# Window attention kernel: the running maxima enter the score matmuls through a free bias row instead of a product of their own

## The reference, cut to what matters

```python
xn = layernorm(x in channels-last)                 # 8 x 32 x 32 pixels, C = 64
win = xn in windows of 8 x 8                       # 128 windows of 64 tokens
q, k, v = (win @ w_qkv + b_qkv) split in 8 heads of depth 8
attn = (q * 8 ** -0.5) @ k.T + rel_bias_table[REL_IDX]   # bias by head, query and key
attn = softmax(attn, axis=-1)                      # over the 64 keys
out = (attn @ v) @ w_proj + b_proj
x1 = x + out, then layernorm, MLP, and the gated convolutions
```

## Time and profile before

| what | value |
|---|---|
| median of 3 runs | 324.87 us (323.93 to 325.02) |
| the profiled execution, its time | 324.21 us |
| its span in the trace | 322.4 us |
| PE busy | 289.2 us, 90% |
| DVE busy | 235.0 us, 73% |
| ACT busy | 203.0 us, 63% |
| POOL busy | 107.3 us, 33% |
| attention steps 0 to 7 | about 33 to 182 us of the span |

### The profile page before, as it was taken

The page is one execution under the profiler, slowest core; times in us unless marked ns, Lnnn a source line. Parts: engine busy times, 40 slices in busy tenths (PEclk is TensorE's granted clock), DMA queues, the critical chain, the costliest instruction groups (busy, mean ns, idle before and its releaser), DMA issues.

```text
span 322.4 us, 6206 instructions
## 1 busy us (share of the span) xinstructions
PE 289.2 (90%) x2314; PEld 211.3 (66%) x2314; DVE 235.0 (73%) x456; ACT 203.0 (63%) x343; POOL 107.3 (33%) x144
## 2 busy tenths in 40 slices
PE   2648979999999999999989797898999999999993
PEld 2236766878878686886868543453577777777772
DVE  4867437589798888979787336679999999976211
ACT  6696633948667685865535788987953746754400
POOL 4151425756576567555441601231310000000000
PEclk9986989999999999999979999999999999999998
DMA  6870383434244333424430000590008659767811
GB/s 162 178 156 31 84 188 85 104 76 90 71 98 89 78 84 76 103 67 96 101 71 2 0 2 0 115 212 14 2 0 169 130 113 196 141 137 147 182 33 33
DMA packets 17276, 29.94 MB, mean 93 GB/s; under 512 B 5536, under 2 KB 12192, under 8 KB 17248
## 3 DMA queue, kind: packets, MB, share of 16 engines
q1 hardware_dynamic: 13792, 22.72, 30.9%
q0 software_dynamic: 2880, 6.03, 11.0%
q10 hardware_dynamic: 576, 0.81, 1.0%
HBM read 4.22 MB, written 2.10 MB: 20 GB/s over the span
## 4 chain that ended last, share of the span: by engine, by line
PE 76%; DVE 7%; ACT 5%; SPq 4%; DMA 4%; issue 2%; POOL 0%; DVEq 0%; ACTq 0%
PE psum L1089 27%; PE psum L868 13%; PE psum L791 5%; PE psum L865 5%; PE psum L884 5%; PE psum L1013 3%; PE psum L844 3%; DVE maxima L1209 3%; SPq L379 3%; PE psum L1001 3%; PE psum L813 3%; DMA k_heads<-k_parts 3%; PE psum L892 2%; PE psum L818 2%; PE psum L823 2%
## 5 line engine op out<-in xcount | busy, mean ns | idle before, releaser
L1089 PE MATMUL psum<-shifted,conv_w 128*128 128x512 f32 x336 | 86.5, 419 | 0.0
L1089 PEld LDWEIGHTS psum<-shifted,conv_w 128*128 128x128 f32 x336 | 63.9, 191 | 21.6 <-issue 1.3
L868 PEld LDWEIGHTS psum<-q_heads,k_blocks 128*128 128x128 f32 x384 | 56.1, 194 | 6.5 <-issue 3.0
L868 PE MATMUL psum<-q_heads,k_blocks 128*128 128x256 f32 x384 | 57.3, 286 | 0.0
L1209 DVE TENSOR_REDUCE maxima<-psum 128x8 f32<-128x512 f32 x64 | 40.1, 683 | 12.2 <-PE psum L844 12.0
L603 ACT ACTIVATE probs<-psum 128x512 f32<-128x512 f32 x64 | 37.5, 603 | 18.2 <-PE psum L868 18.0
L461 POOL DMA_DIRECT2D k_blocks<-k_parts x56 | 32.2, 583 | 11.5 <-PE psum L868 11.5
L865 PE MATMUL psum<-minus_max,pick 128*128 128x512 f32 x64 | 32.7, 511 | 0.5 <-ACT probs L603 0.3
L844 PE MATMUL psum<-k_heads,q_blocks 128*128 128x256 f32 x128 | 24.0, 314 | 9.5 <-DMA k_heads<-k_parts 6.9
L791 PE MATMUL psum<-parts,center_average 128*128 128x512 f32 x64 | 22.6, 436 | 8.7 <-DVE parts L287 7.1
L287 POOL TENSOR_TENSOR parts<-x,parts 128x256 fp32r<-128x256 f32 (+1 forms) x21 | 19.4, 938 | 32.0 <-ACT parts L552 22.2
(11 more groups left out here) (142 smaller groups left out, 468.1 us busy)
## 6 DMA issues: line engine op xcount, KB each, us to landing
shifted<-images SPq DMA_DIRECT2D x32, 332.5 KB, 5.5
q_heads<-q_parts SPq DMA_DIRECT2D x128, 32.0 KB, 2.2
k_blocks<-k_parts POOLq DMA_DIRECT2D x56, 64.0 KB
k_heads<-k_parts SPq DMA_DIRECT2D x64, 32.0 KB, 2.3
out<-x SPq DMA_DIRECT2D x8, 256.0 KB, 4.8
q_blocks<-q_parts POOLq DMA_DIRECT2D x28, 64.0 KB, 2.5
x<-in_x SPq DMA_DIRECT2D x6, 256.0 KB, 6.2
x<-in_x SPq DMA_DIRECT2D x4, 128.0 KB, 4.0
```

The source lines that it names most:

```text
L868: ins = pe.matmul(bank[:, hh * G // 2:(hh + 1) * G // 2], k_blocks[:, hh, w // (NW // 2), k_part, w % (NW // 2), :], of_half(q_heads[:, q_ ...
L1089: ins = pe.matmul(psum[:, CONV0 + bh, :], conv_w[bh][:, w_part, t, :], img[:, y:y + H - 1:2, x0:x0 + W], start=t == 0 and w_part + part == ...
```

## The change

Of each bias row the bias of the last key is subtracted (from all keys alike, for each query), on both sides: in the rows for the maximum pass and in those for the scores. The row of the last key is then zero and is not needed. It holds the maxima of the query now, rounded to the format of the matmul operands, with weights of -1, 0 and 1 in `k_blocks`, such that each half of the 128 keys gets minus its own batch's maximum.

- The `pick` matmul of each `scores` and its constant are gone, and so are `maxima_t` and `minus_max`.
- The maxima are transposed in two halves of four window pairs: 32 columns each. The first transpose stands ahead of maximum pass 6, the second where the only one stood. DVE rounds either half into `gauge` by one copy of 32x128 (after the fifth maximum, and after the eighth).
- `send_gauge` places a half by two DMAs, 16 pieces of 512 bytes each, into the one free row of either half of `q_heads`. ACT issues the first half's after exponential 7, POOL the second half's after the second `key_blocks`. scores(g, 0) and scores(g, 4) wait for them.
- `q_heads` and `q_parts` have another order in memory: high and low part of a window pair lie side by side, so that a piece of a query DMA is one of 2048 bytes and not two of 1024.
- In the start there is one more load, `rel_base`: the base biases for all 128 partitions, in 1024 pieces of 256 bytes, 256 KB, on SP's queue ahead of the raw weights. DVE subtracts them (one instruction more, and one changed from a copy to a subtraction). POOL's making of `pick` is replaced by four small memsets.

```diff
+def _key_rows():
+    r = ((_p % T)[:, None] == T - 1 - _p % T).astype(np.float32)
+    r[_p % T == 0] = -(_p >= T).astype(np.float32)
+    return r
...
+        def maxima_bank(s):
+            return psum[0:32, MAX0, 0:128] if s else psum[0:32, PV, 256:384]
...
-        def reversal():
-            return const("reverse").unsqueeze(1).to_broadcast([128, NW, 128])
+        def reversal(name="reverse"):
+            return const(name).unsqueeze(1).to_broadcast([128, NW, 128])
+        FREE_ROWS = ((0, T), (1, 0))
+        def send_gauge(engine, n, s):
+            engine.wait_ge(S["dv_gauge"], 2 * n + s + 1)
+            if isinstance(n, int) and n == 0:
+                engine.wait_ge(S[f"q_heads_set{s}"], 1 + s)
+            else:
+                engine.wait_ge(S["pe_scores"], NW * (n - 1) + (s + 1) * NW // 2)
+            for hh, row in FREE_ROWS:
+                engine.dma_start(q_heads[row:row + 1, s, heads_of(hh)].rearrange("o h w l t -> o (h w) (l t)").bitcast(F32),
+                                 gauge[hh * 16:(hh + 1) * 16, s, :].bitcast(F32)).then_inc(S[f"gauge_in{s}"], 16)
...
             load_bias(1, "rel_table")
+            sp.dma_start(rel_base.rearrange("p (a f) -> p a f", a=WS), bass.AP(d["rel_table"].tensor, d["rel_table"].offset, [[0, 128], [side * NH, WS], [1, WS * NH]])
+                         ).then_inc(S["rel_in1"], 16)
...
                 sp.wait_ge(S["dv_q_low"], n + 1)
-                some = slice(half * G // 2, (half + 1) * G // 2)
+                some = slice(half * NW // 2, (half + 1) * NW // 2)
                 for h in range(NH):
-                    sp.dma_start(of_head(q_heads, h)[:, :, h, some].bitcast(F32), of_head(q_parts, h)[:, n % 2, :, some].bitcast(F32)
+                    sp.dma_start(of_head(q_heads, h)[:, half, h].rearrange("p w l t -> p (w l t)").bitcast(F32), of_head(q_parts, h)[:, n % 2, some].rearrange("p w l t -> p (w l t)").bitcast(F32)
...
             pool.memset(gaps[:], 0.0).then_inc(S["zeroed"], 1)
-            pool.wait_ge(S["consts_in"], 16)
-            pool.wait_ge(S["center_in"], 16)
-            pool.tensor_tensor(pick[:], const("average").unsqueeze(1).to_broadcast([128, NW, 128]),
-                               const("window_of_row").unsqueeze(2).to_broadcast([128, NW, 128]), ALU.mult).then_inc(S["po_pick"], 1)
+            pool.wait_ge(S["k_blocks_zeroed"], 1)
+            pool.wait_ge(S["zeroed"], 1)
+            for hh, row in FREE_ROWS:
+                for bh, sign in ((0, -1.0), (1, 1.0)):
+                    if hh + bh > 0:
+                        pool.wait_ge(S["key_rows_set"], 2 * hh + bh)
+                    pool.memset(k_blocks[row:row + 1, hh, :, 1, :, bh * T:(bh + 1) * T].bitcast(F32), sign).then_inc(S["key_rows_set"], 1)
...
                     key_blocks(nxt, 1 - par, 1)
+                    send_gauge(pool, nxt, 1)
...
             low_of_next_x(2)
+            send_gauge(pool, 0, 1)
...
                 exponentials(g, 7)
+                if nxt is not None:
+                    send_gauge(act, nxt, 0)
...
             late_bias(1, rel_low)
+            send_gauge(act, 0, 0)
...
-            def transpose_maxima(n):
-                pe.wait_ge(S["dv_max"], NW * (n + 1))
-                pe.matmul(psum[0:C, MAX0, 0:128], maxima[:], const("ident"), start=True, stop=True).then_inc(S["pe_maxt"], 1)
+            def transpose_maxima(n, s):
+                pe.wait_ge(S["dv_max"], NW * n + (s + 1) * NW // 2)
+                if s == 0 and not (isinstance(n, int) and n == 0):
+                    pe.wait_ge(S["dv_turned"], 2 * n - 1)
+                pe.matmul(maxima_bank(s), maxima[:, s * 32:(s + 1) * 32], const("ident"), start=True, stop=True).then_inc(S["pe_maxt"], 1)
-                if w == 0:
-                    pe.wait_ge(S["dv_minus"], g + 1)
                     pe.wait_ge(S["k_blocks_in0"], 64 * (g + 1))
+                    if isinstance(g, int) and g == 0:
+                        pe.wait_ge(S["key_rows_set"], 4)
                     pe.wait_ge(S[f"q_heads_in{w // (NW // 2)}"], 16 * NH * (g + 1))
+                    pe.wait_ge(S[f"gauge_in{w // (NW // 2)}"], 32 * (g + 1))
                 bank = psum[:, PROB0 + w % 2, :]
-                pe.matmul(bank, pick[:, w, :], minus_max[:, :, :], start=True, stop=False)
                         ins = pe.matmul(bank[:, hh * G // 2:(hh + 1) * G // 2], k_blocks[:, hh, w // (NW // 2), k_part, w % (NW // 2), :],
-                                        of_half(q_heads[:, q_part], hh)[:, :, w * T:(w + 1) * T], start=False, stop=hh + k_part == 2)
+                                        q_heads[:, w // (NW // 2), heads_of(hh), w % (NW // 2), q_part, :],
+                                        start=k_part + q_part == 0, stop=k_part == 1)
-            def weighted_values(g, quad, par):
+            def weighted_values(g, quad, par, nxt=None):
+                if quad == 1 and nxt is not None:
+                    pe.wait_ge(S["dv_gauge"], 2 * nxt + 1)
...
                         for w in windows:
+                            if w == 6:
+                                transpose_maxima(nxt, 0)
...
                 if nxt is not None:
-                    transpose_maxima(nxt)
+                    transpose_maxima(nxt, 1)
                     variance2(prev)
-                weighted_values(g, 1, par)
+                weighted_values(g, 1, par, nxt)
...
             for w in range(NW):
+                if w == 6:
+                    transpose_maxima(0, 0)
             queries(1)
-            transpose_maxima(0)
+            transpose_maxima(0, 1)
             keys(1)
-            pe.wait_ge(S["po_pick"], 1)
...
-            def high_of_bias(n, rel, done):
-                dve.wait_ge(S[f"rel_in{n}"], 32)
-                dve.tensor_copy(rel.rearrange("p (h a b) -> p h a b", h=NH, a=WS), patches(n)).then_inc(S[done], 1)
-                dve.wait_ge(S[done], 1)
-            def low_of_bias():
-                high, low = (t.rearrange("p (h a b) -> p h a b", h=NH, a=WS) for t in (rel_high.bitcast(F32), rel_low))
-                dve.tensor_tensor(low, patches(1), high, ALU.subtract).then_inc(S["dv_rel_low"], 1)
+            def square_rows(t):
+                return t.rearrange("p (h a b) -> p h a b", h=NH, a=WS)
+            def keys_bias():
+                dve.wait_ge(S["rel_in0"], 32)
+                rows = patches(0)
+                dve.tensor_tensor(square_rows(rel_flipped), rows, rows[:, :, WS - 1:WS, WS - 1:WS].to_broadcast([128, NH, WS, WS]),
+                                  ALU.subtract).then_inc(S["dv_rel_flipped"], 1)
+                dve.wait_ge(S["dv_rel_flipped"], 1)
+            def queries_bias():
+                dve.wait_ge(S["rel_in1"], 48)
+                dve.tensor_tensor(square_rows(rel_whole), patches(1), rel_base.rearrange("p (a b h) -> p h a b", a=WS, b=WS),
+                                  ALU.subtract).then_inc(S["dv_rel_whole"], 1)
+                dve.wait_ge(S["dv_rel_whole"], 1)
+                dve.tensor_copy(rel_high, rel_whole).then_inc(S["dv_rel_high"], 1)
+                dve.wait_ge(S["dv_rel_high"], 1)
+                low_part(dve, rel_whole, rel_high, rel_low).then_inc(S["dv_rel_low"], 1)
...
                 dve.wait_ge(S["ac_q_high"], n + 1)
-                dve.scalar_tensor_tensor(q_parts[:, par, 1, :], psum[:, MISC0, :], q_bias[:, 0:1],
-                                         q_parts[:, par, 0, :].bitcast(F32), ALU.add, ALU.subtract).then_inc(S["dv_q_low"], 1)
+                dve.scalar_tensor_tensor(q_parts[:, par, :, 1, :], by_window(psum[:, MISC0, :]), q_bias[:, 0:1],
+                                         q_parts[:, par, :, 0, :].bitcast(F32), ALU.add, ALU.subtract).then_inc(S["dv_q_low"], 1)
                 dve.wait_ge(S["pe_max"], NW * n + w + 1)
-                dve.tensor_reduce(maxima[:, w * NH:(w + 1) * NH], max_bank(w).rearrange("p (h t) -> p h t", t=T),
+                dve.tensor_reduce(maxima[:].rearrange("p (s h w) -> p s w h", s=2, h=NH)[:, w // (NW // 2), w % (NW // 2), :], max_bank(w).rearrange("p (h t) -> p h t", t=T),
-            def spread_maxima(n):
-                dve.wait_ge(S["pe_maxt"], n + 1)
-                dve.tensor_scalar(maxima_t[0:C, :], psum[0:C, MAX0, 0:T], -1.0, None, ALU.mult)
-                dve.tensor_scalar(maxima_t[C:128, :], psum[0:C, MAX0, T:2 * T], -1.0, None, ALU.mult).then_inc(S["dv_maxt"], 1)
-                dve.wait_ge(S["dv_maxt"], n + 1)
-                dve.tensor_tensor(minus_max[:], maxima_t[:].unsqueeze(1).to_broadcast([128, NH, T]),
-                                  const("head_of_row").unsqueeze(2).to_broadcast([128, NH, T]), ALU.mult).then_inc(S["dv_minus"], 1)
+            def round_maxima(n, s):
+                dve.wait_ge(S["pe_maxt"], 2 * n + s + 1)
+                if not (isinstance(n, int) and n == 0):
+                    dve.wait_ge(S[f"gauge_in{s}"], 32 * n)
+                dve.tensor_copy(gauge[0:32, s, :], maxima_bank(s)).then_inc(S["dv_gauge"], 1)
...
```

(14 more changed lines are left out.)

33 lines of the change are left out of this document (17 added, 16 removed).

## The result

| what | before | after |
|---|---|---|
| median of the runs (20 of each) | 323.75 us | 323.68 us (319.16 to 325.55) |
| ratio | | 0.9942, 95% [0.9915, 0.997] |
| the profiled execution, its time | 324.21 us | 320.28 us |
| its span | 322.4 us | 318.5 us |
| PE busy | 289.2 us | 280.9 us |

Ratios leave out executions more than 1.5% above the fastest of the same kernel: six of the twenty here (324.00 to 325.55 us; with them the means are 322.90 and 324.02 us, 0.35% apart), two of six in the second measurement, one without the base load, and one of 1419 us without the gauge DMAs.

What follows compares the result with a forecast made beforehand. PE and DVE were taken as one loop bounding each step, PE nearly alone. Steps save 7.7 us, the start costs 1.3: 324.2 - 7.7 + 1.3 = 317.8 profiled, plus 0.66 gives a 318.4 us median; range 311.8 to 322.5.

Steps and rivals of the forecast that it cites:

- so 0.9 are saved: Whole step, PE up to the weighted values: five products gone, 1.15 us, less 0.25 given back because ACT limits the scores.
- the five products' 1.15: PE between keys product and weighted values in a whole step: five removed products at 0.23 us each.
- ACT's copy of the residual: Whole step: normalising waits for ACT's residual copy and deviation; residual 0.84 us earlier, so normalising starts at about 13.21.
- the 1.45 us that I gave to steps 0 and 1: Gains of the first two steps: 0.35 us in step 0, behind the last key DMA, and 1.1 in step 1.
- I took 0.66 as before: Whole kernel: the median lies 0.66 us above the profiled execution, so 317.8 becomes 318.4 us.
- The base load: Start: 256 KB on SP's queue delay the first key DMAs and all behind them; cost 1.3 us, bounds 0 to 1.54.
- The gauge DMAs: Steps: ACT's two issues, at most 1.2 us, fit its 1.69 us of idle time ahead of the keys copy; no cost.
- The late-gauge rival: First half lands after 4.4 us, scores 0 start 1.5 us late in seven steps; 325.5 us, about no change; chance 0.05.
- DVE's copies: Steps, on DVE: two copies of 32x128 replace the three spreading instructions, 0.25 us each, bounds 0.22 and 0.69.
- Steps 6 and 7: Last two steps: 1.3 us net saved in step 6, where nothing is normalised, and 1.6 in step 7, which runs on PE.
- The clock rival: PE's clock falls in its longer pauses, about 1.7 us lost in each of six steps; 328.5 us, slower; chance 0.11.
- a wait of 0.7 ahead of the fourth pass: Sign in the steps: PE waits about 0.7 us for DVE's first maximum ahead of its fourth maximum pass.

Runs made afterwards that it cites:

- second measurement: The changed kernel run once more, unedited, for a second profile: median 321.26 us, ratio 0.9874 [0.9817, 0.9932].
- low part on DVE: Changed kernel with the low part of the far group's square made by DVE, ahead of the residual, instead of by POOL: ratio 0.9872 [0.984, 0.9905].
- early loads: SP's four loads of x's last half moved into its pause between the first queries' halves: old kernel 0.9933, 321.49 us; changed kernel 0.9901, 320.35 us.
- the squares first: Changed kernel with ACT's squares of the far group ahead of exponential 1 instead of behind it: ratio 0.9916 [0.9885, 0.9946].
- x_ahead: Changed kernel with the four loads for the last half of x issued by ACT in idle time instead of by SP: ratio 0.9882 [0.9847, 0.9916].

## Why the prediction was right and wrong

**The step that failed** is "so 0.9 are saved; the turning starts at 11.88. DVE is free by 11.17, so PE still sets this point". Nothing was saved there: the turning starts at 12.84 (12.78 before), and DVE is free at 99.76 - 88.19 = 11.57. Two things were wrong in it.

*A wait that I had not looked for.* The variance, two matmuls ahead of the weighted values, needs POOL's low part of the squares, which needs ACT's squares behind the value copy. The page pointed away from it (POOL 0% of the chain, and no wait of the variance). The slack of this wait in the kernel of before was 118.79 - (117.11 + 1.29) = 0.39 us, which would have been the first warning. But the slack does not give the result either: POOL's start moved up by 0.25 with the value copy, and with its 1.28 it would have ended at 10.41, ahead of the 10.58 at which PE comes when nothing holds it (table). POOL ended at 10.95 because DVE's second half of the low part now started 0.01 us before it. The same meeting takes 0.67 from DVE's residual. I had no term for the meeting at all: in the kernel of before it lay on DVE's low part alone, 1.81 for 0.69, and I took that as the length of DVE's work.

*A term of the wrong size.* I gave back 0.25 of the five products' 1.15 for ACT. With POOL out of the way the weighted values come at 11.24: 0.37 is saved and 0.78 given back. The value copy, and the exponentials behind it, start only 0.26 earlier.

The measured table, us behind the keys product:

| | before | forecast | after | after, low part on DVE |
|---|---|---|---|---|
| variance of far | 11.06 | | 11.01 | 10.58 |
| weighted values | 11.61 | 10.7 | 11.67 | 11.24 |
| their turning | 12.78 | 11.88 | 12.84 | 12.41 |
| normalising | 14.01 | 13.21 | 13.68 | 13.25 |
| fifth maximum | 17.54 | 16.47 | 17.06 | 16.55 |
| next keys | 18.97 | 18.15 | 18.68 (18.57 to 18.76) | 18.17 |

From normalising on, the forecast holds to 0.1 in the last column. Its way up to there does not even then (11.24, not 10.7); normalising came on time because its other term, ACT's copy of the residual, was right: with POOL out the residual starts at 10.44, 0.81 earlier than before.

In us: the profiled execution took 320.28 for a forecast of 317.8, and the 2.0 that the whole steps lack are the most of these 2.5. The median missed by 5.3 (323.68 for 318.4). The other 2.8 are its larger distance from the profiled execution, and their cause stays open in the main.

**The first steps.** In the profile shown their sum is what was forecast (0.2 for 0.15), by luck: step 0 gained 19.56 - 18.01 = 1.55 for 0.35, as the last of the second key DMAs landed in 2.66 us instead of 4.68, and step 1 only 18.22 - 18.09 = 0.13 for 1.1. There PE waited 0.59 for the first half's gauge DMA, and its first scores started 4.06 behind keys. In the other executions with the loads of x in place the end of step 1 stands at 69.91 to 72.10 in the changed kernel and its edits, and at 69.78, 69.95 and (without the products) 70.81 in the old one and its edits; there the 1.45 us that I gave to steps 0 and 1 are lost, to k_heads and the gauge. The median of the changed kernel lies 3.4 us above its profiled execution, where I took 0.66 as before; if its executions are spread like these, up to 2.5 of this stand in these places, and the rest isn't seen, as only profiled executions show places. The chain of the start, for comparison with the earlier trace rows:

```profile
21.41 4.61 DMA k_heads<-k_parts
...
42.71 2.66 DMA k_heads<-k_parts
```

**The base load.** First key landing 26.02 against 24.66: 1.36, forecast 1.3. This is one pair of executions; over all the first maximum pass starts at 24.5 to 25.9 without the load and at 25.7 to 27.9 with it. The size was right, but the row that I took it from is not what I read in it: the earlier trace rows has 6.03 MB in 2880 packets, 2.1 KB each in the mean, and not pieces of 256 bytes. In the trace of after the load is 1024 packets of 256 bytes and 22.8 ns each, 1.46 us on sixteen engines. The Trainium skill, "DMA: Bandwidth & Descriptors", Specifications, wants 512 bytes a piece for line rate; by that I had named 1.54 as the dear end, and the trace is a little below it; no run here has the same load in longer pieces.

**The gauge DMAs.** Hidden in whole steps, as forecast: ACT's issues end at 87.48 + 1.17 = 88.65, ahead of the key copy at 89.33, and nothing waits for their landing. The group by line:

```profile
L347 ACTq DMA_DIRECT2D q_heads<-gauge x16: 510/567/789, 31.4 to 160.6; - x16
L347 POOL DMA_DIRECT2D q_heads<-gauge x16: 507/508/511, 34.2 to 163.4; - x16
```

The late-gauge rival (0.05) came only in the first steps: 0.59 us in step 1 of the profile shown, 2.4 at the longest where the loads were early. It cost those steps at most these waits, and never 7 us.

**DVE's copies** took 0.27 and 0.28 (forecast 0.25). **Steps 6 and 7** gave 31.47 - 28.08 = 3.4 (forecast 2.9), but partly by the clock: in the profiled execution of before it was 0.50 from 166 to 169 us, and in that of after not until 175.6. Two executions in which it fell in neither step can be compared from the keys product to the first matmul of the MLP: 178.50 - 143.04 = 35.46 (kernel of before with early loads) and 177.68 - 144.67 = 33.01 (second measurement), 2.45 us less. Nothing is normalised there, and the chain through the variance of far is absent. In the profiled execution of before this stretch took 181.98 - 145.67 = 36.31, so the fall cost 0.85 there, and I had put it at 1.7.

**The clock rival** did not come in whole steps: 1.00 in the earlier trace rows and 1.00 now, with PE's idle time at 1.1 us. The Trainium skill, "TensorE: Matmul & The Clock Gate", A second HAM failure mode, speaks of many short pauses that let the clock fall again and again; no whole step here shows it. It came once, at the end of step 7, and cost 3.02 - 1.70 = 1.3 up to the MLP. "The tail of the kernel hangs on the last step and moves with it" was wrong by that.

**Signs.** Right: the lines gone, the first pass later by 1.3, no wait for q_heads in whole steps. Wrong: keys 18.1 to 18.2 apart; a wait of 0.7 ahead of the fourth pass (none; 0.57 with the squares first); DVE's wait ahead of the turning was 1.27, not 0.7, since PE was late; the first pass of step 0 came at 45.51, not 46.5.

**What stays open:** the longer step behind the loop (18.76 for 18.60, but not without the gauge DMAs, and not in x_ahead, which has them); why executions of the changed kernel scatter by 6 us (319.16 to 325.55) where those of before scatter by 4; and whether the clock or the start makes the most of that, as only profiled executions show either.

## What to carry to other kernels

A gain on one engine passes as far as its next wait for another, also a wait that is zero today: for every wait between the edit and the point that sets the end, subtract the end of the releaser from the start of the waiter. Follow the releasers back to where they really start, as here to a copy that only one of five removed products preceded. The smallest slack, and what the releaser itself gains, bound what can pass.

Then look for instructions that take longer in a step than elsewhere, here 2.52 us for 1.40. They may be waiting inside for another engine, and an edit that moves either of the two by a few hundredths of a us can turn round which one waits. An off-path engine with a small-looking operation (POOL, 0% of the chain) can so be the next bound. Its subtraction held DVE for 1.12 us before, and done by DVE itself it takes 0.69; moving it took 0.4 us more off a whole step, more than the change itself had (0.3).
